# Gathering the chosen rows at the end of the ranking stage instead of at the start of the transformer stage

## The chip, the cores and the metric

The kernel runs on one core of a Trainium2 chip. The metric is the device time of one execution in microseconds (us). The program is one launch that runs seven stages one after the other. Names used below: PE is TensorE, DVE is VectorE, ACT is ScalarE, POOL is GpSimd, and SP is SyncE, which only issues DMAs here.

## What is computed

Input x is 4 batches of 1024 tokens of 1024 features, all float32. Two blocks are applied.

```python
x = x + tanh(g_xattn) * mamba(ctx, z=_layernorm(x))        # a selective scan
x = x + tanh(g_ffn) * mixture_of_depths(_layernorm(x))
# inside mixture_of_depths:
scores = einsum('btd,d->bt', hidden_states, w_router)
_, idx = top_k(scores, k)            # k = 128 of the 1024 tokens of a batch
idx = sort(idx)
sel = hidden_states[b, idx]          # 4 x 128 rows
...                                  # rotary attention at positions idx, MLP, gate
output = hidden_states.at[b, idx].set(gated)
```

So each batch ranks its tokens, the 128 best of each batch go through one transformer layer (16 query heads, 8 key heads of 128, causal over all 512 chosen rows), and their results are written back to their places. Every other row gets only the layer norm part.

## The kernel before

The stages, in order, are `project_stage`, `scan_stage` for batches 0 and 1, `route_stage` and `layer_stage` for batches 0 and 1 (`first = 0`), `scan_stage` for batches 2 and 3, and `route_stage` and `layer_stage` for batches 2 and 3 (`first = 2`). Each stage is a block in which every engine has a program of its own, written out by hand; engines meet only at semaphores. A stage ends when all five engines have come to its end: the code between two stages is a barrier of all engines, and no instruction or DMA of the next stage is issued ahead of it. SP is the last of them here, since its program ends with waits for all DMAs of the stage. This kernel therefore has two places, called boundaries below, at which a ranking stage hands over to a transformer stage.

`route_stage` (names with `r_`) reads the rows of both batches (`r_x`), computes each row's score, and ranks by comparing: `rank(b, a)` on DVE counts for 128 tokens how many scores of the batch are larger, `choose(b)` marks those with fewer than 128. `place(b)` gives each chosen token its slot (a PE product `p_sums`, then four small dependent DVE operations), `choose_slots(b)` builds eight 128x128 selection matrices `pick[:, a]` on DVE (in `first = 0` they lie in a part of `t_hidden`), and PE multiplies them with the positions held in `counts`, adding up in `p_pos` the sorted positions of the 128 chosen tokens, one on each partition. `copy_pos(b)` copies them to `r_pos`. The positions of batch b = 0 of the stage are done within the ranking of b = 1. Those of b = 1 are the stage's last work: SP waits for them, writes them to a scratch tensor in HBM and waits for that store.

`layer_stage` (names with `l_`) starts by loading the positions back (`l_pos`), then small tables, the router row and `tg` (the two gates), and then the weight ring `l_ring`, all from SP in that order:

```python
sp.dma_start(pos[:], t["pos"][:, 0:KEYS]).then_inc(pos_in, 16)
for dst, src in ((cols, t["cols"]), (swap, t["swap"]), (router, t["router"].partition_broadcast(P)),
                 (tg, t["g"].partition_broadcast(P))):
    sp.dma_start(dst[:], src).then_inc(small, 16)
```

DVE turns the positions into int32 row numbers (`from_i` for rows of this stage, `row_i` for the final write, `pos_i` for the rotary table). POOL waits for all three (`idx_ready, 3`) and issues four indirect DMAs: two gather 128 rows of 4 KB each (`l_rows`), two gather 128 rows of 1 KB each of the rotary table (`l_ropes`). DVE takes statistics of the rows (L1883), POOL raises them to the power -1/2 (L1646), ACT normalises (L1783, after a tanh of `tg` that stands ahead of it, L1780), PE transposes (L1675), ACT and DVE copy the transposed tiles out (L1790, L1900, which need `cols`), and PE begins the query and key products (L1686), each of 24 weight tiles of 512 KB. From there the layer is a long row of PE products.

Of the kernel before, what the change touches and what calls it, by code (L numbers as in the profile page):

```python
# [24 lines left out]
P = 128  # L25
# [13 lines left out]
SPAN = 2  # L39
# [22 lines left out]
class Through:  # L62

    def __init__(self, nc, ctx):
        self.hidden = ctx.enter_context(nc.sbuf_tensor("t_hidden", [P, NI, ROWS], F32))

class Kept:

    def __init__(self, nc, ctx, through):
        self.hidden = through.hidden
# [1005 lines left out]
def route_stage(nc, t, ctx, keep, first):  # L1079
# [34 lines left out]
    pos = sb("pos", [P, SPAN])  # L1114
# [12 lines left out]
    if late:  # L1127
# [3 lines left out]
        w_x = sb("w_x", [P, NE, ND])  # L1131
# [9 lines left out]
    slots, pick_ready, pos_sums, pos_done = (sem(n) for n in ("slots", "pick_r", "pos_sums", "pos_done"))  # L1141

# [6 lines left out]
    with nc.Block() as block:  # L1149
        @block.sync  # L1150
        def _(sp):
# [57 lines left out]
        def _(pool):  # L1209
# [72 lines left out]
        def _(pe):  # L1282
# [42 lines left out]
            for b in range(SPAN):  # L1325
# [15 lines left out]
        def _(dve):  # L1341
# [113 lines left out]
def layer_stage(nc, t, ctx, keep, first):  # L1455
# [22 lines left out]
    rows = sb("rows", [P, SPAN, DI])  # L1478
# [14 lines left out]
    ropes = sb("ropes", [P, SPAN, 2 * DH])  # L1493
# [28 lines left out]
    small, made, pos_in, idx_ready, k0_in, v0_in = (sem(n) for n in ("small", "made", "pos_in", "idx", "k0_in", "v0_in"))  # L1522
    x_in, rope_in = ([sem(f"{n}_in{b}") for b in range(SPAN)] for n in ("x", "rope"))
# [28 lines left out]
    with nc.Block() as block:  # L1552
        @block.sync
        def _(sp):
            sp.dma_start(pos[:], t["pos"][:, 0:KEYS]).then_inc(pos_in, 16)
# [73 lines left out]
        def _(pool):  # L1629
# [25 lines left out]
            if last_half:  # L1655
                for b in range(NB):
# [10 lines left out]
        def _(pe):  # L1667
# [30 lines left out]
            for r in range(2):  # L1698
                for b in range(SPAN):
                    if r == 0:  # L1700
                        pe.wait_ge(rope_in[b], 16)
                    last = nc.tensor.transpose(acc[3][:, r * ROWS + b * P:r * ROWS + (b + 1) * P], ropes[:, b, r * DH:(r + 1) * DH], ident[:])
# [165 lines left out]
        def _(dve):  # L1868
            dve.wait_ge(pos_in, 16)
            nc.vector.tensor_copy(pos_i[:], pos[:]).then_inc(idx_ready, 1)  # L1870
            for b in range(KEYS):
                nc.vector.tensor_scalar(row_f[:, b:b + 1], pos[:, b:b + 1], float(b * L), None, ALU.add)
            for b in range(SPAN):
                last = nc.vector.tensor_scalar(from_f[:, b:b + 1], pos[:, first + b:first + b + 1], float(b * L), None, ALU.add)
            last.then_inc(stat_chain, 1)
            dve.wait_ge(stat_chain, 1)
            nc.vector.tensor_copy(from_i[:], from_f[:]).then_inc(idx_ready, 1)
            nc.vector.tensor_copy(row_i[:], row_f[:]).then_inc(idx_ready, 1)

            for b in range(SPAN):  # L1880
                dve.wait_ge(x_in[b], 16)
                for h in range(H2):
                    nc.vector.bn_stats(stats[:, b, 6 * h:6 * h + 6], halves(rows[:, b], h)).then_inc(stat_chain, 1)  # L1883
            for b in range(SPAN):
                dve.wait_ge(stat_chain, 1 + H2 * (b + 1))
# [53 lines left out]

            dve.wait_ge(rope_ready, 1)  # L1940
# [81 lines left out]
SCRATCH = dict(pre=(SPAN * NE * P, L), ug=(STEPS * P, 2 * L), xd=(NB * ND, L), x2_0=(SPAN * L, DI), x2_2=(SPAN * L, DI), pos=(P, NB), k0=(P, NKV * ROWS), v0=(P, SPAN * DI),  # L2022
               h2T0=(P, KT * ROWS), base0=(ROWS, DI), coef0=(P, SPAN), mlp0=(ROWS, DI))
SCRATCH_KIND = "Internal"
STAGES = ((project_stage,), (scan_stage, 0), (route_stage, 0), (layer_stage, 0), (scan_stage, SPAN))
# [73 lines left out]
```

## Time and profile before

| | us |
|---|---|
| median of 3 runs | 2959.4 (2956.54 to 2963.68) |
| the profiled execution's own time | 2957.47 |
| its span, first to last recorded instruction | 2955.7 |
| PE busy | 2411.5 (82%) |
| DVE busy | 2043.6 (69%) |
| ACT busy | 1637.1 (55%) |
| POOL busy | 1637.4 (55%) |
| DMA, mean of the span | 142 GB/s |

All trace times are counted from the start of the span. The busy shares are means over stages with different limits, so what a change at one boundary is worth is read in the stretch around it. The first ranking stage ends near 1099 us, the second near 2331 us.

### The profile page before, as it was taken

What the parts mean: (1) busy time and instruction counts of PE and PEld (TensorE: products, weight loads), DVE (VectorE), ACT (ScalarE), POOL (GpSimd) and SP (SyncE); (2) the same over time, 40 slices, a digit from 0 to 9 for tenths busy, and PEclk for the clock granted to TensorE, in tenths of its full rate; (3) what the DMA queues carried; (4) which work ended last, traced back from release to release, by engine and by line L of the source; (5) the groups of instructions that cost most, each with busy time, mean ns of one, the idle gap of its engine ahead of it and who ended that gap; (6) DMA issues with size and microseconds to landing.
All of it is one profiled execution on the core that took longest, in us unless ns stands there. A gap on an engine that the chain in (4) does not pass through costs nothing. (4 is left out here: it accounts for less than half of the span.)

```text
span 2955.7 us, 33859 instructions
## 1 busy us (share of the span) xinstructions
PE 2411.5 (82%) x11576; PEld 1657.1 (56%) x11576; DVE 2043.6 (69%) x2562; ACT 1637.1 (55%) x3494; POOL 1637.4 (55%) x728
## 2 busy tenths in 40 slices
PE   8858778787777548986888888887886699999998
PEld 3335555555555317554666666666553486568863
DVE  4559999999999754433998999999996533210000
ACT  3468888888888342244887777887772213310000
POOL 1169999999999410004998998998991100000000
PEclk9979999999999768997999999999997799999999
DMA  6722252342522486744226325325326742244442
GB/s 262 239 88 75 65 162 79 105 138 65 164 65 61 181 343 225 281 146 149 90 80 196 97 92 177 100 90 185 95 63 264 261 135 79 68 143 153 150 156 100
DMA packets 237818, 418.62 MB, mean 142 GB/s; under 512 B 34512, under 2 KB 118736, under 8 KB 234832
## 3 DMA queue, kind: packets, MB, share of 16 engines
q1 hardware_dynamic: 224144, 360.36, 37.7%
q10 hardware_dynamic: 12160, 51.39, 4.3%
q0 software_dynamic: 1344, 4.72, 0.4%
q8 instruction: 93, 1.52, 0.2%
q14 instruction: 77, 0.63, 0.1%
HBM read 332.52 MB, written 83.89 MB: 141 GB/s over the span
## 5 line engine op out<-in xcount | busy, mean ns | idle before, releaser
L629 POOL TENSOR_TENSOR s_x<-s_du,k_bB 128x2048 f32<-128x2048 f32 (+1 forms) x256 | 882.0, 3458 | 29.9 <-issue 23.2
L705 PE MATMUL s_py<-k_ident,s_x 128*128 128x128 f32 x4096 | 564.1, 283 | 181.0 <-DVE s_x L1010 104.7
L705 PEld LDWEIGHTS s_py<-k_ident,s_x 128*128 128x128 f32 x4096 | 478.9, 145 | 401.4 <-DVE s_x L1010 179.4
L956 ACT ACTIVATE s_pA<-s_delta,k_negA 128x512 f32<-128x512 f32 x768 | 500.2, 681 | 184.4 <-DVE s_x L1010 179.3
L636 POOL TENSOR_TENSOR s_x<-s_hp,k_bC 128x1024 f32<-128x1024 f32 x192 | 452.9, 2373 | 26.6 <-DVE s_hp L1029 26.5
L1686 PE MATMUL l_p<-l_hT,l_ring 128*128 128x256 f32 x1792 | 397.2, 381 | 2.4 <-DVE l_hT L1900 1.4
L1010 DVE TENSOR_TENSOR s_x<-s_pA,k_bC 128x1024 f32<-128x1024 f32 x320 | 384.4, 1201 | 4.6 <-DMA k_bC<-scratch_xd 4.4
L1686 PEld LDWEIGHTS l_p<-l_hT,l_ring 128*128 128x128 f32 x1792 | 342.1, 191 | 50.2 <-issue 2.0
L856 ACT ACTIVATE s_xT<-s_duT,k_BT 128x128 f32<-128x128 f32 x1024 | 335.9, 387 | 0.1
L1029 DVE TENSOR_TENSOR_SCAN s_pA<-s_pA,s_x 128x512 f32<-128x512 f32 x256 | 302.4, 1215 | 40.3 <-ACT s_pA L956 40.1
L1029 DVE TENSOR_TENSOR_SCAN s_pA<-s_pA,s_carry,s_x 128x512 f32<-128x512 f32 x256 | 316.5, 1270 | 0.3
L694 PE MATMUL s_pA<-k_ident,s_xT 128*128 128x128 f32 x1024 | 152.6, 297 | 93.8 <-DVE s_hp L1029 90.3
L1693 PE MATMUL l_p<-l_ring,t_hidden 128*128 128x512 f32 x512 | 220.2, 592 | 0.0
L1654 POOL TENSOR_TENSOR l_squares<-l_squares,l_minus_half 128x1 f32<-128x1 f32 x4 | 2.2, 548 | 382.0 <-DVE l_squares L1990 382.0
L694 PEld LDWEIGHTS s_pA<-k_ident,s_xT 128*128 128x128 f32 x1024 | 122.7, 151 | 148.8 <-DVE s_hp L1029 146.9
L1663 POOL DMA_INDIRECT out_dram<-l_rows,l_row_i x2 | 1.9, 952 | 331.1 <-DVE l_rows L2017 331.1
L956 ACT ACTIVATE s_x<-s_delta,k_negA 128x512 f32<-128x512 f32 x256 | 169.8, 708 | 0.0
L1693 PEld LDWEIGHTS l_p<-l_ring,t_hidden 128*128 128x128 f32 x512 | 97.1, 190 | 121.1 <-issue 121.0
L1029 DVE TENSOR_TENSOR_SCAN s_hp<-s_pA,s_carry,s_x 128x512 f32<-128x512 f32 x128 | 161.9, 1265 | 4.2 <-ACT s_pA L956 4.2
L2012 DVE TENSOR_TENSOR t_hidden<-l_silu,l_p 128x256 f32<-128x256 f32 x32 | 13.5, 421 | 208.4 <-PE l_p L1686 208.4
L1029 DVE TENSOR_TENSOR_SCAN s_hp<-s_pA,s_x 128x512 f32<-128x512 f32 x128 | 154.8, 1209 | 1.9 <-ACT s_pA L956 0.6
L755 PE MATMUL s_p_in<-t_hidden,s_w_in 128*128 128x512 f32 x256 | 136.7, 617 | 0.0
(213 smaller groups left out, 3721.8 us busy)
## 6 DMA issues: line engine op xcount, KB each, us to landing
k_bC<-scratch_xd SPq DMA_DIRECT2D x32, 1024.0 KB, 9.5
scratch_ug<-p_ug ACTq DMA_DIRECT2D x16, 1024.0 KB, 3.9
k_u<-scratch_ug SPq DMA_DIRECT2D x64, 256.0 KB, 3.4
k_bB<-scratch_xd SPq DMA_DIRECT2D x16, 1024.0 KB, 9.2
s_gy<-scratch_ug SPq DMA_DIRECT2D x64, 256.0 KB, 4.4
s_xt<-in_x SPq DMA_DIRECT2D x64, 256.0 KB, 4.7
scratch_x<-s_xt SPq DMA_DIRECT2D x64, 256.0 KB, 2.3
r_x<-scratch_x SPq DMA_DIRECT2D x32, 512.0 KB, 12.5
```

The lines of the kernel that those rows point to most:

```text
L629: pool.tensor_tensor(out=x[:, 4 * g:4 * g + many], in0=du[:, s % 2:s % 2 + 1].broadcast_to([P, many, HALF]), in1=bB[:, 3 * g + g % 2:3 * g ...
L636: pool.tensor_tensor(out=x[:, 2 * i:2 * i + 2], in0=hp[:, POOL_PAIRS.index(i)], in1=bC[:, 2 * i:2 * i + 2], op=ALU.mult).then_inc(pool_hc, 1)
L694: last = nc.tensor.transpose(pA[:, n % 4, a * P:(a + 1) * P], xT[:, k, a * P:(a + 1) * P], ident[:])
L705: last = nc.tensor.matmul(py[:, a], x[:, n, a * P:(a + 1) * P], ident[:], is_transpose=True, start=False, stop=is_last and a == HALF // P - 1)
L755: last = nc.tensor.matmul(p_in[:], w_in[:, s % 2, i], ctxT[:, chunk(s) % 2, i], start=i == 0, stop=i == NK - 1)
L856: last = nc.scalar.activation(xT[:, k, a * P:(a + 1) * P], duT[:, a * P:(a + 1) * P], ACT.Copy, scale=BT[:, chunk(s) % 2, k, a:a + 1])
L956: nc.scalar.activation(out, delta[:, s % 2], ACT.Exp, scale=negA[:, s % NE, n:n + 1]).then_inc(dA_ready, 1)
L1010: nc.vector.tensor_tensor(x[:, 2 * i:2 * i + 2], pA[:, j:j + 2], bC[:, 2 * i:2 * i + 2], ALU.mult).then_inc(vec_hc, 1)
L1029: nc.vector.tensor_tensor_scan(out, dA, added, initial, ALU.mult, ALU.add).then_inc(scanned, 1)
L1686: last = nc.tensor.matmul(out[:, 0:ROWS], w[:, c * P:(c + 1) * P], src[:, c], start=c == 0, stop=c == KT - 1)
L1693: last = nc.tensor.matmul(banks[2 * a + h][:], src[:, a * P:(a + 1) * P], w[:, h * HALF:(h + 1) * HALF], start=is_first, stop=is_last)
L2012: nc.vector.tensor_tensor(hidden[:, m], silu[:, m % 2], acc[2 + m % 2][:, 0:ROWS], ALU.mult).then_inc(act_ready, 1)
```

## The change

The gathers move from the start of `layer_stage` to the end of `route_stage`, and their results live in tensors that both stages share.

- A class `Chosen` allocates `rows` and `ropes` (names `c_rows`, `c_ropes`) for each pair of a ranking and a transformer stage. `layer_stage` uses them in place of its own.
- The positions of all batches stay in SBUF, in `t_pos`. The scratch tensor, SP's store of it and SP's load of it are gone.
- `copy_pos(b)` makes the row numbers itself: one operation becomes four on DVE, and the second of them waits for the first.
- POOL's program in `route_stage` gets, for each batch, a wait for `from_i` and the gather of the rows, and a wait for `pos_i` and the gather of the rotary rows. SP waits for all four at the stage's end.
- Each of the eight selection matrices raises `pick_ready` by itself, and PE waits for each one ahead of its product, where it had waited for all eight.
- In the last stage the row numbers of the final write are made on DVE after `coefficients()`'s definition and ahead of the wait for the rotary table; before, they were made at the start of both transformer stages.
- `w_x` of the first ranking stage moves into a free part of `t_hidden`.

```diff
+class Chosen:
+    def __init__(self, nc, ctx, first):
+        self.rows = ctx.enter_context(nc.sbuf_tensor(f"c{first}_rows", [P, SPAN, DI], F32))
+        self.ropes = ctx.enter_context(nc.sbuf_tensor(f"c{first}_ropes", [P, SPAN, 2 * DH], F32))
...
 # route_stage, SP
-            sp.wait_ge(pos_done, SPAN)
-            sp.dma_start(t["pos"][:, first:first + SPAN], pos[:]).then_inc(small, 16)
-            sp.wait_ge(small, 64)
+            for b in range(SPAN):
+                sp.wait_ge(gathered[b], 32)
...
 # route_stage, POOL
+            for b in range(SPAN):
+                pool.wait_ge(idx_ready, b + 1)
+                pool.indirect_dma_start(out=chosen_rows.rows[:, b], out_offset=None, in_=t[f"x2_{first}"],
+                                        in_offset=bass.IndirectOffsetOnAxis(ap=from_i[:, b:b + 1], axis=0)).then_inc(gathered[b], 16)
+                pool.wait_ge(pos_done, b + 1)
+                pool.indirect_dma_start(out=chosen_rows.ropes[:, b], out_offset=None, in_=t["rope"],
+                                        in_offset=bass.IndirectOffsetOnAxis(ap=pos_i[:, b:b + 1], axis=0)).then_inc(gathered[b], 16)
...
 # route_stage, PE
-                pe.wait_ge(pick_ready, b + 1)
                 if b:
                     pe.wait_ge(pos_done, b)
                 for a in range(TILES):
+                    pe.wait_ge(pick_ready, TILES * b + a + 1)
                     last = nc.tensor.matmul(p_pos[:], pick[:, a], counts[:, P + a:P + a + 1], start=a == 0, stop=a == TILES - 1)
...
 # route_stage, DVE
             def choose_slots(b):
                 dve.wait_ge(slots, 4 * b + 4)
+                if b:
+                    dve.wait_ge(pos_sums, b)
                 for a in range(TILES):
-                    last = nc.vector.tensor_scalar(pick[:, a], counts[:, 0:P], slot[:, a:a + 1], chosen[:, b, a:a + 1],
-                                                   ALU.is_equal, ALU.mult)
-                last.then_inc(pick_ready, 1)
+                    nc.vector.tensor_scalar(pick[:, a], counts[:, 0:P], slot[:, a:a + 1], chosen[:, b, a:a + 1],
+                                            ALU.is_equal, ALU.mult).then_inc(pick_ready, 1)
             def copy_pos(b):
                 dve.wait_ge(pos_sums, b + 1)
-                nc.vector.tensor_copy(pos[:, b:b + 1], p_pos[:]).then_inc(pos_done, 1)
+                nc.vector.tensor_scalar(from_f[:, b:b + 1], p_pos[:], float(b * L), None, ALU.add).then_inc(from_ready, 1)
+                dve.wait_ge(from_ready, b + 1)
+                nc.vector.tensor_copy(from_i[:, b:b + 1], from_f[:, b:b + 1]).then_inc(idx_ready, 1)
+                nc.vector.tensor_copy(pos[:, first + b:first + b + 1], p_pos[:])
+                nc.vector.tensor_copy(pos_i[:, b:b + 1], p_pos[:]).then_inc(pos_done, 1)
...
 # layer_stage, SP, POOL, DVE
-            sp.dma_start(pos[:], t["pos"][:, 0:KEYS]).then_inc(pos_in, 16)
...
-            pool.wait_ge(idx_ready, 3)
-            for b in range(SPAN):
-                pool.indirect_dma_start(out=rows[:, b], out_offset=None, in_=t[f"x2_{first}"],
-                                        in_offset=bass.IndirectOffsetOnAxis(ap=from_i[:, b:b + 1], axis=0)).then_inc(x_in[b], 16)
-            for b in range(SPAN):
-                pool.indirect_dma_start(out=ropes[:, b], out_offset=None, in_=t["rope"],
-                                        in_offset=bass.IndirectOffsetOnAxis(ap=pos_i[:, first + b:first + b + 1], axis=0)).then_inc(rope_in[b], 16)
...
-            dve.wait_ge(pos_in, 16)
-            nc.vector.tensor_copy(pos_i[:], pos[:]).then_inc(idx_ready, 1)
...
+            if last_half:
+                for b in range(KEYS):
+                    last = nc.vector.tensor_scalar(row_f[:, b:b + 1], pos[:, b:b + 1], float(b * L), None, ALU.add)
+                last.then_inc(row_chain, 1)
+                dve.wait_ge(row_chain, 1)
+                nc.vector.tensor_copy(row_i[:], row_f[:]).then_inc(row_chain, 1)
             dve.wait_ge(rope_ready, 1)
```

The instructions move as follows. First DVE, at the first boundary, from the last selection matrices on. Before (the two branches are the end of one stage and the start of the next; the matrices go to a part of `t_hidden`):

```order
L1404 TENSOR_SCALAR t_hidden<-r_counts,r_slot,r_chosen 128x128 x8
L1410 COPY r_pos<-r_ppos 128x1
L1149 UNCONDITIONAL_BRANCH
L1867 UNCONDITIONAL_BRANCH
L1870 CAST l_pos_i<-l_pos 128x2
L1872 TENSOR_SCALAR l_row_f<-l_pos 128x1 x2
L1874 TENSOR_SCALAR l_from_f<-l_pos 128x1 x2
L1877 CAST l_from_i<-l_from_f 128x2
L1878 CAST l_row_i<-l_row_f 128x2
L1883 BN_STATS l_stats<-l_rows 128x6 x4
```

And with the change:

```order
L1425 TENSOR_SCALAR t_hidden<-r_counts,r_slot,r_chosen 128x128 x8
L1430 TENSOR_SCALAR r_from_f<-r_ppos 128x1
L1432 CAST r_from_i<-r_from_f 128x1
L1433 COPY t_pos<-r_ppos 128x1
L1434 CAST r_pos_i<-r_ppos 128x1
L1162 UNCONDITIONAL_BRANCH
L1876 UNCONDITIONAL_BRANCH
L1880 BN_STATS l_stats<-c_rows 128x6 x4
```

The row numbers are now made ahead of the two branches, and the statistics L1880 are the first DVE work of the transformer stage; the `l_row` operations are gone from this stage.

Second, POOL at the same boundary, from the last work of the ranking stage (the power of the variances) on. Before:

```order
L1224 TENSOR_TENSOR r_rstd<-r_var,r_minus_half 128x8 x2
L1149 UNCONDITIONAL_BRANCH
L2033 ISA
L1628 UNCONDITIONAL_BRANCH
L1630 MEMSET l_minus_half 128x4
L1631 MEMSET l_ident 128x128
L1632 MEMSET l_causalT 128x128
L1634 AFFINE_SELECT l_ident<-l_ident 128x128
L1636 AFFINE_SELECT l_causalT<-l_causalT 128x128
L1640 DMA l_rows<-scratch_x_0,l_from_i 128x1024 x2
L1643 DMA l_ropes<-in_rope,l_pos_i 128x256 x2
L1646 TENSOR_TENSOR l_roots<-l_roots,l_minus_half 128x4
```

And with the change:

```order
L1236 TENSOR_TENSOR r_rstd<-r_var,r_minus_half 128x8 x2
L1239 DMA c_rows<-scratch_x_0,r_from_i 128x1024
L1242 DMA c_ropes<-in_rope,r_pos_i 128x256
L1239 DMA c_rows<-scratch_x_0,r_from_i 128x1024
L1242 DMA c_ropes<-in_rope,r_pos_i 128x256
L1162 UNCONDITIONAL_BRANCH
L2033 ISA
L1645 UNCONDITIONAL_BRANCH
L1647 MEMSET l_minus_half 128x4
L1648 MEMSET l_ident 128x128
L1649 MEMSET l_causalT 128x128
L1651 AFFINE_SELECT l_ident<-l_ident 128x128
```

The four indirect DMAs now stand ahead of the barrier (the ISA row), with the rotary rows of a batch behind its own rows; the `l_` memsets and L1656 follow one another without a DMA between.

## Rows read from the trace of the kernel before

**Rows 1.** Chain that ended last, second boundary: start us, us, what.

```profile
2331.07 1.98 DMA l_pos<-scratch_pos
...
2334.16 1.05 POOL l_rows L1640
2335.20 0.30 issue
2335.51 9.72 DMA l_rows<-scratch_x,l_from_i
...
2345.25 1.29 DVE l_stats L1883 x2
...
2348.51 1.25 ACT l_normed_rows L1783
...
2354.72 7.14 PE l_p L1686 x32
```

**Rows 2.** Timeline, first boundary: start us, us, engine, line, operation.

```profile
1088.18 0.15 DVE L1410 COPY r_pos<-r_ppos 128x1 f32<-128x1 f32 x1
...
1089.80 0.17 DVE L1395 TENSOR_TENSOR_SCAN r_upto<-r_ones,r_sums 128x8 f32<-128x8 f32 x1
1090.00 0.17 DVE L1397 TENSOR_TENSOR r_slot<-r_upto,r_sums 128x8 f32<-128x8 f32 x1
...
1090.41 2.14 DVE L1404 TENSOR_SCALAR t_hidden<-r_counts,r_slot,r_chosen 128x128 f32<-128x128 f32 x8
...
1092.60 3.58 PE L1337 MATMUL r_ppos<-r_counts,t_hidden 128*128 128x1 f32 x16 [3.05 <-DVE t_hidden L1404]
...
1096.40 0.32 SPq L1197 DMA_DIRECT2D scratch_pos<-r_pos  x1
...
1099.05 0.32 SPq L1555 DMA_DIRECT2D l_pos<-scratch_pos  x1
...
1100.83 0.48 SPq L1558 DMA_DIRECT2D l_tg<-in_g  x1
...
1105.12 0.20 ACT L1780 ACTIVATE l_tg<-l_tg 128x2 f32<-128x2 f32 x1 [15.84 <-DMA l_tg<-in_g]
...
1111.29 1.29 DVE L1883 BATCH_NORM_STATS2 l_stats<-l_rows 128x6 f32<-128x512 f32 x2 [9.98 <-DMA l_rows<-scratch_x,l_from_i]
1113.86 1.29 DVE L1883 BATCH_NORM_STATS2 l_stats<-l_rows 128x6 f32<-128x512 f32 x2 [1.28 <-DMA l_rows<-scratch_x,l_from_i]
...
1117.11 2.37 ACT L1783 ACTIVATE l_normed_rows<-l_rows,l_shift,l_roots 128x1024 f32<-128x1024 f32 x2 [11.78 <-DVE l_shift L1893]
...
1123.32 5.05 PE L1686 MATMUL l_p<-l_hT,l_ring 128*128 128x256 f32 x21 [0.33 <-DVE l_hT L1900]
```

**Rows 3.** Timeline, end of the second ranking stage.

```profile
2324.66 3.58 PE L1337 MATMUL r_ppos<-r_counts,r_pick 128*128 128x1 f32 x16 [3.05 <-DVE r_pick L1404]
...
2328.46 0.34 SPq L1197 DMA_DIRECT2D scratch_pos<-r_pos  x1
```

**Rows 4.** Busy time by stretch: stretch, engines, granted clock, DMA share, GB/s.

```profile
1094.00:1096.00 2.00, 2.00 (x11) 2.00 (x10) 0.00 (x0) 0.00 (x0) 0.00 (x0) 0.50 0.00 0
1106.00:1108.00 2.00, 0.00 (x0) 0.00 (x0) 0.00 (x0) 0.00 (x0) 0.56 (x1) 0.50 1.02 418
```

**Rows 5.** DMA issues, 1095 to 1130 us: KB each, median us to landing.

```profile
l_rows<-scratch_x,l_from_i POOLq DMA_INDIRECT x2, 10.2
l_ropes<-in_rope,l_pos_i POOLq DMA_INDIRECT x2, 10.1
...
scratch_pos<-r_pos SPq DMA_DIRECT2D x1, 1.0 KB, 1.4
...
l_tg<-in_g SPq DMA_DIRECT2D x1, 1.0 KB, 4.3
```

**Rows 6.** Tile l_ring, first six loads of layer 0.

```profile
DMA to landing us min/median/max: 6.4/10.7/13.1
```

**Rows 7.** DMA issues, last 11 us of the span.

```profile
out_dram<-l_rows,l_row_i POOLq DMA_INDIRECT x2, 3.4
```

More of the change, by code:

```diff
@@ L66, in __init__ @@
         self.hidden = ctx.enter_context(nc.sbuf_tensor("t_hidden", [P, NI, ROWS], F32))
+        self.pos = ctx.enter_context(nc.sbuf_tensor("t_pos", [P, NB], F32))
+class Chosen:
+    def __init__(self, nc, ctx, first):
+        self.rows = ctx.enter_context(nc.sbuf_tensor(f"c{first}_rows", [P, SPAN, DI], F32))
+        self.ropes = ctx.enter_context(nc.sbuf_tensor(f"c{first}_ropes", [P, SPAN, 2 * DH], F32))
 class Kept:
     def __init__(self, nc, ctx, through):
-        self.hidden = through.hidden
+        self.hidden, self.pos = through.hidden, through.pos
         def sb(name, shape):
@@ L1076, with route_stage @@
 DOWN_PARTS = (14, 26)
-def route_stage(nc, t, ctx, keep, first):
+def route_stage(nc, t, ctx, keep, chosen_rows, first):
     TILES, BUFS = L // P, SPAN * L // P
@@ L1113, in route_stage @@
     slot = sb("slot", [P, TILES])
-    pos = sb("pos", [P, SPAN])
+    pos = keep.pos
+    from_f = sb("from_f", [P, SPAN])
+    from_i = ctx.enter_context(nc.sbuf_tensor(f"r{first}_from_i", [P, SPAN], I32))
+    pos_i = ctx.enter_context(nc.sbuf_tensor(f"r{first}_pos_i", [P, SPAN], I32))
     p_row = [ctx.enter_context(nc.psum_tensor(f"r{first}_prow{j}", [P, L], F32)) for j in range(2)]
@@ L1130, in route_stage @@
         pick = space[:, (LATE_BUFS + 1) * L:(LATE_BUFS + 2) * L].rearrange("p (a c) -> p a c", c=P)
-        w_x = sb("w_x", [P, NE, ND])
+        w_x = space[:, (LATE_BUFS + 2) * L:(LATE_BUFS + 2) * L + NE * ND].rearrange("p (e c) -> p e c", c=ND)
         xd = space[:, LATE_BUFS * L:LATE_BUFS * L + SPAN * HALF].rearrange("p (b l) -> p b l", b=SPAN)
@@ L1141, in route_stage @@
     slots, pick_ready, pos_sums, pos_done = (sem(n) for n in ("slots", "pick_r", "pos_sums", "pos_done"))
+    from_ready, idx_ready, gathered = sem("from_r"), sem("idx_r"), [sem(f"gathered{b}") for b in range(SPAN)]
     def buf(k):
@@ L1452, with layer_stage @@
 LATE, LATE_FROM, LATE_QK = 4, 4, 10
-def layer_stage(nc, t, ctx, keep, first):
+def layer_stage(nc, t, ctx, keep, chosen_rows, first):
     QK = NH + NKV
@@ L1476, in at_least @@
             eng.wait_ge(s, n)
-    rows = sb("rows", [P, SPAN, DI])
+    rows, ropes, pos = chosen_rows.rows, chosen_rows.ropes, keep.pos
     hid = sb("hid", [P, SPAN, DI])
@@ L1520, in layer_stage @@
     acc, side = banks[0:4], banks[4:8]
-    small, made, pos_in, idx_ready, k0_in, v0_in = (sem(n) for n in ("small", "made", "pos_in", "idx", "k0_in", "v0_in"))
-    x_in, rope_in = ([sem(f"{n}_in{b}") for b in range(SPAN)] for n in ("x", "rope"))
+    small, made, row_chain, k0_in, v0_in = (sem(n) for n in ("small", "made", "row_chain", "k0_in", "v0_in"))
     stat_chain, means, var_ready, roots_ready, shift_ready = (sem(n) for n in ("stat", "means", "var", "roots_r", "shift_r"))
@@ L1655, in _ @@
             if last_half:
+                pool.wait_ge(row_chain, 2)
                 for b in range(NB):
@@ L1868, in _ @@
         def _(dve):
-            dve.wait_ge(pos_in, 16)
-            nc.vector.tensor_copy(pos_i[:], pos[:]).then_inc(idx_ready, 1)
-            for b in range(KEYS):
-                nc.vector.tensor_scalar(row_f[:, b:b + 1], pos[:, b:b + 1], float(b * L), None, ALU.add)
             for b in range(SPAN):
[L1874 to L1881, printed above, removed]
                 for h in range(H2):
@@ L2020, in _, with run, choose_and_attend @@
                         last.then_inc(rows_ready, 1)
-SCRATCH = dict(pre=(SPAN * NE * P, L), ug=(STEPS * P, 2 * L), xd=(NB * ND, L), x2_0=(SPAN * L, DI), x2_2=(SPAN * L, DI), pos=(P, NB), k0=(P, NKV * ROWS), v0=(P, SPAN * DI),
+SCRATCH = dict(pre=(SPAN * NE * P, L), ug=(STEPS * P, 2 * L), xd=(NB * ND, L), x2_0=(SPAN * L, DI), x2_2=(SPAN * L, DI), k0=(P, NKV * ROWS), v0=(P, SPAN * DI),
                h2T0=(P, KT * ROWS), base0=(ROWS, DI), coef0=(P, SPAN), mlp0=(ROWS, DI))
 SCRATCH_KIND = "Internal"
-STAGES = ((project_stage,), (scan_stage, 0), (route_stage, 0), (layer_stage, 0), (scan_stage, SPAN))
-LAST_STAGES = ((route_stage, SPAN), (layer_stage, SPAN))
 def build(nc, t):
-    def run(stages, keep):
-        for stage, *which in stages:
-            with nc.cleanup_on_exit(), ExitStack() as ctx:
-                stage(nc, t, ctx, keep, *which)
+    def run(stage, *args):
+        with nc.cleanup_on_exit(), ExitStack() as ctx:
+            stage(nc, t, ctx, *args)
+    def choose_and_attend(keep, first):
+        with ExitStack() as half:
+            chosen_rows = Chosen(nc, half, first)
+            run(route_stage, keep, chosen_rows, first)
+            run(layer_stage, keep, chosen_rows, first)
     with ExitStack() as whole:
@@ L2038, in build @@
         with ExitStack() as outer:
-            run(STAGES, Kept(nc, outer, through))
-        run(LAST_STAGES, through)
+            keep = Kept(nc, outer, through)
+            run(project_stage, keep)
+            run(scan_stage, keep, 0)
+            choose_and_attend(keep, 0)
+            run(scan_stage, keep, SPAN)
+        choose_and_attend(through, SPAN)
 def kernel(x, ctx_1024, g_xattn, g_ffn, L0_xattn_in_proj_w, L0_xattn_conv_w, L0_xattn_conv_b, L0_xattn_x_proj_w,
```

9 lines of the change are left out of this document (1 added, 8 removed).

## The prediction

> **What bounds the kernel now.** I read the chain of work that ended last first, because the busy shares are means over seven unlike stages. At the second boundary [rows 1] the reader is to see that it runs through no busy engine: the position load, the making of row numbers, POOL's first gather and the wait for the second, then statistics, normalisation, and at 2354.72 PE's query products. From the stage's start at 2331.07 to there are 23.65 us, 9.72 of them one gather. The timeline of the first boundary [rows 2] shows the same: SP's position load at 1099.05, statistics at 1111.29 and 1113.86 (the second waited for its gather), L1686 at 1123.32, which is 24.27 us. Everything behind these two points follows from them: each boundary has one chain, each stage waits for the stage before, so what a boundary gains the span gains.
>
> The gathers are slow in company. Their median from issue to landing is 10.2 us for rows of 4 KB and 10.1 us for rows of 1 KB [rows 5]; a quarter of the bytes took as long, while the DMA engines moved 418 GB/s [rows 4] with the weight ring queued beside them. The final scatter, 512 KB by the same kind of issue and alone, landed in 3.4 us [rows 7].
>
> **The change part by part.** Call S the start of the transformer stage, E the end of the position products of b = 1, and S' and E' the same points with the change.
>
> *The position products.* PE needed 3.58 us for its 8 products of b = 1 at both boundaries [rows 2, 3], at the lower clock (granted 0.50, that is 1.2 GHz, after a stretch without work) [rows 4]; that is 0.45 us each. DVE makes eight matrices in 2.14 us, 0.27 each [rows 2], so PE sets the pace once it may follow. It starts after the first matrix, some 0.3 us, instead of after 2.14: 1.8 us gained. Seven more waits cost between nothing and what PE took after the last matrix (1092.55 to 1092.60, 0.05 each, 0.35 together); I take nothing, since a wait whose matrix is ready long before holds nobody.
>
> *The longer `copy_pos(0)`.* It stands between the ranking and `choose(1)` on DVE at 1088.18, on the chain. One copy becomes four operations. The second depends on the first, and such a step took 0.20 us (1089.80 to 1090.00) [rows 2]; each of the other two costs between nothing and the copy's 0.15. I take 0.4 us in all. So E' = E − 1.8 + 0.4 = E − 1.4.
>
> *The gathers of b = 0* are issued from about 1089 on, five us ahead of those of b = 1. DVE and PE work covers them; their 640 KB last 1.5 us at 418 GB/s. Without that cover they would cost what those of b = 1 do.
>
> *From E' to the stage's end.* First two DVE steps, 0.4 us, then 0.3 us until POOL issues, as between its issues [rows 1], then the row gather, which held POOL 1.05, another 0.3, then the rotary gather: issued at E' + 2.05. SP waits for its landing, D later. The barrier took 1.25 us: the store of the positions, at 1096.40, landed 1.4 later, at 1097.8, and the stage began at 1099.05 [rows 2, 5]. S' = E' + 3.3 + D. Before, S was 2.87 after E (1092.60 + 3.58 to 1099.05), and 2.83 at the second boundary, where the store at 2328.46 follows in the same way [rows 2, 3]. Together, S' − S = D − 0.95.
>
> *D* has no row, since no gather ran alone. From below, a 1 KB store landed in 1.4 us; from above, the gathers took 10.1 beside the weights [rows 5]. The nearest row is the scatter's 3.4 [rows 7], and 384 KB less at 418 GB/s take off 0.9. The barrier forbids any weight load beside it, so I take 2.8 us, between the two. Then S' = S + 1.85. The rows of b = 1, issued 1.35 earlier, land first even at 3.4.
>
> The Trainium skill has a price for such a DMA ("DMA: Bandwidth & Descriptors", Anatomy of one DMA): about 2.0 us and the bytes at 436 GB/s. By it D is 2.3, the forecast 1 us lower, and the trace agrees with it for the scatter (3.2 against 3.4). It disagrees with 10.1 for a gather, unless company explains that.
>
> *From S' to the query products.* The rows are there. Statistics of two tiles take two times 1.29 less a small overlap [rows 2], 2.5; from their end to the normalisation were 1.97 (2346.54 to 2348.51) [rows 1]. So ACT has its scale at S' + 4.6. But ACT's tanh of `tg` stands ahead of it in ACT's order: this is late next. `tg` was issued at 1100.83, 1.78 after S, the fifth issue; it becomes the fourth, 0.36 earlier. It lands 4.3 later [rows 5], at S' + 5.7; with 0.2 for the tanh, ACT normalises at S' + 6.0. I keep 4.3, since the router row, not the gathers, is queued ahead of it. From there to L1686 were 6.21 us at both boundaries [rows 1, 2]; those are dependent steps of PE, ACT and DVE, and stay. L1686 starts at S' + 12.2.
>
> The weights must be there too. SP issues the first at about S' + 1.9; the earliest of the first six landed after 6.4 us [rows 6], at S' + 8.3. It is covered by 3.9 us. Behind it, PE takes 3.57 us for a tile (7.14 for two) [rows 1] and 512 KB take 1.25 us at 418 GB/s, so the ring keeps ahead, in the last stage as well, where 4 MB of kept tensors follow.
>
> *At nothing:* the `row_f` and `row_i` operations in the last stage, six small ones while DVE waits for PE and ACT; the allocation of `w_x`.
>
> *Sum.* First boundary 24.27 − 12.2 − 1.85 = 10.2 us; second 23.65 − 12.2 − 1.85 = 9.6 us. Together 19.8 us. The profiled execution took 2957.5 us, so 2937.7; the median of the three runs is 1.9 above it, which gives 2939.6. I forecast 2939.
>
> **The rivals.**
>
> *A gather is slow by itself (7%).* For it: the two sizes landed alike. Against it: the scatter, and the 418 GB/s beside it. With D = 10.1, S' is 9.15 us later than S, the boundaries give 2.9 and 2.3 us, and the time is 2954, which this measurement can hardly tell from before (it tells 0.2%, 5.9 us).
>
> *Weights become the last to arrive (8%).* If the first tile landed as late as the slowest of six, 13.1 us [rows 6], L1686 would start at S' + 15.0, 2.8 later at each boundary: 2945. Against it: less is queued ahead of it than before.
>
> *POOL and DVE hold each other up (8%).* POOL's gathers of b = 0 now stand beside DVE's placing and its eight matrices. If DVE stood still for each of two POOL issues of 1.05 us [rows 1], `choose` to E' grows by up to 2.1 us at each boundary: 2944. For it speaks no row, since POOL gathered only while DVE was idle. The Trainium skill ("SBUF — State Buffer", SBUF: two separate sides) says that the two engines share a port pair that one holds for a whole instruction, and that such DVE work keeps POOL from writing descriptors. In the second form only the gathers of b = 0 are late, which are covered; no run here shows either yet.
>
> *Slower (3%).* SP's wait for the last rotary gather now stands ahead of the barrier, and behind it are queued all table and weight loads. Before, a late gather had these beside it. The gain of a boundary is 12.1 us less S' − S, so it is gone at D = 13, and D = 16 gives about 2965. Longer landings than 10.1 in an emptied machine would need a cost that no row shows.
>
> *Another cause (4%)*, such as the moved addresses of tensors in the scan stages: no row prices it; I spread it over all three.
>
> **How the numbers follow.** The forecast has 70%. Its own range: D from 1.4 to 3.4 moves it by −2.8 to +1.2, the landing of `tg` by 1 us at each boundary, the waits on PE by +0.7, and the median of three runs by some 3: 2934 to 2944. With the weights and the POOL case, 86% lie from 2933 to 2948, which is the range; I leave out the slow gather. Faster by over 0.2% is 0.87 (these three and a part of the last), within 0.2% 0.09, slower 0.04.
>
> **What would show it.** In the profile after: the position products beginning some 0.4 us after the first matrix and lasting about 3.6; a rotary gather landing near 2.8 us, with the next stage starting about 1.25 behind it, near 1100.9; statistics within 0.2 us of that start; a tanh near S' + 5.8 as ACT's last wait before the normalisation; L1686 near 1113.1 and 2345. The prediction is wrong if D is far above 3.4, if L1686 waits for the ring, or if the scan stages change their length.

## The result and the profile after

The changed kernel took 2937.9 us, median of 5 runs (2934.8 to 2944.8), against 2957.8 for the kernel before on the same chip (2955.5 to 2963.7). The ratio is 0.993, 95% interval 0.9914 to 0.9947: 20.7 us less, somewhere from 15.7 to 25.4. The forecast was 2939. The profiled execution took 2935.34 us.

The page of the profile after, its span and its busy row:

```profile
span 2933.6 us, 33860 instructions
PE 2400.6 (82%) x11576; PEld 1647.5 (56%) x11576; DVE 2043.5 (70%) x2563; ACT 1636.6 (56%) x3494; POOL 1636.5 (56%) x728
```

The busy time of DVE, ACT and POOL hardly moved; 22.1 us of span are gone. PE's busy time is 10.9 us shorter here (it was 2411.5), but in a second trace of the same kernel (e0, below) it is 2410.0 with nearly the same span, 2935.3, so that is not the gain. It was waiting that went, and the timeline of the first boundary shows which (start us, us, engine, line, operation, in brackets the idle time before and what ended it):

```profile
1088.01 0.15 DVE L1430 TENSOR_SCALAR r_from_f<-r_ppos 128x1 f32<-128x1 f32 x1
1088.19 0.15 DVE L1432 CAST r_from_i<-r_from_f 128x1 int32<-128x1 f32 x1
...
1088.39 0.16 DVE L1408 TENSOR_SCALAR r_chosen<-r_larger 128x8 f32<-128x8 f32 x1
...
1090.13 0.95 POOL L1242 DMA_INDIRECT c_ropes<-in_rope,r_pos_i  x1 [0.30 <-issue]
...
1090.48 2.14 DVE L1425 TENSOR_SCALAR t_hidden<-r_counts,r_slot,r_chosen 128x128 f32<-128x128 f32 x8
...
1090.97 3.54 PE L1356 MATMUL r_ppos<-r_counts,t_hidden 128*128 128x1 f32 x16 [1.35 <-DVE t_hidden L1425]
...
1095.17 0.94 POOL L1239 DMA_INDIRECT c_rows<-scratch_x,r_from_i  x1 [4.09 <-DVE r_from_i L1432]
1096.41 0.95 POOL L1242 DMA_INDIRECT c_ropes<-in_rope,r_pos_i  x1 [0.30 <-issue]
1101.42 0.10 POOL L1647 MEMSET l_minus_half<- 128x4 f32 x1 [4.06 <-POOLq L2033]
...
1101.46 2.47 DVE L1880 BATCH_NORM_STATS2 l_stats<-c_rows 128x6 f32<-128x512 f32 x4 [6.43 <-PEq L2033]
...
1102.75 0.58 SPq L1575 DMA_DIRECT2D l_tg<-in_g  x1
...
1105.63 0.23 DVE L1890 SCALAR_TENSOR_TENSOR l_shift<-l_mv,l_roots 128x2 f32<-128x2 f32 x2 [1.16 <-POOL l_roots L1656]
1107.33 0.20 ACT L1789 ACTIVATE l_tg<-l_tg 128x2 f32<-128x2 f32 x1 [19.57 <-DMA l_tg<-in_g]
1107.44 2.36 ACT L1792 ACTIVATE l_normed_rows<-c_rows,l_shift,l_roots 128x1024 f32<-128x1024 f32 x2
...
1113.64 6.71 PE L1697 MATMUL l_p<-l_hT,l_ring 128*128 128x256 f32 x30 [1.01 <-DVE l_hT L1897]
```

L1880, L1792 and L1697 are the statistics, the normalisation and the query products, which were L1883, L1783 and L1686 [rows 2]. The transformer stage now starts 2.4 us later (1101.42 against 1099.05), but the statistics begin 0.04 us behind its start instead of 12.24, and the products begin 9.7 us earlier. From the stage's start to the products are 12.22 us instead of 24.28.

The DMA issues of 1094.6 to 1101 us, the two gathers of `b = 1` (median us to landing), and one row of those of 1101 to 1106:

```profile
c_rows<-scratch_x,r_from_i POOLq DMA_INDIRECT x1, 4.2
c_ropes<-in_rope,r_pos_i POOLq DMA_INDIRECT x1, 3.7
```
```profile
l_tg<-in_g SPq DMA_DIRECT2D x1, 1.0 KB, 4.6
```

A rotary gather of 128 KB that took 10.1 us beside the weights [rows 5] lands in 3.7. The chain that ended last of 2309 to 2336 us, the second boundary, answers to [rows 1]:

```profile
2324.64 4.14 DMA l_tg<-in_g
...
2328.80 0.20 ACT l_tg L1789
2329.01 1.14 ACT l_normed_rows L1792
...
2335.11 0.89 PE l_p L1697 x3
```

The gather that filled this chain for 9.72 us is out of it, and the landing of `tg` is in it, as the prediction said.

To account for the time I use marks of the traces. "Chosen" is the start of L1389 (after: L1408) for `b = 1`; "product" is the end of its position products; "start" is the stage's first instruction; "query" is the first query product.

| us, first / second boundary | chosen to product | product to start | start to query | chosen to query |
|---|---|---|---|---|
| before | 7.88 / 7.46 | 2.86 / 2.83 | 24.28 / 23.65 | 35.02 / 33.94 |
| after | 6.12 / 6.27 | 6.91 / 6.87 | 12.22 / 11.80 | 25.25 / 24.94 |

The sums fall by 9.77 and 9.00 us. The longer `copy_pos(0)`, ahead of "chosen", takes 0.26 of each back, so the boundaries gave 18.2 of the 22.1 us of span. The rest lies elsewhere: 0.2 ahead of the first boundary, 1.2 between the two, 2.5 behind the second. The 1.2 is within the scatter: the stretch from the first boundary's query products to the second "chosen" took from 1193.7 (e5) to 1200.7 us (e7) in the traces below. For the 2.5, busy time by stretch (PE, PEld, DVE, ACT, POOL, then granted clock, DMA share, GB/s) of nearly the same place in the last stage, and of the low clock in it, before and after:

```profile
2600.00:2650.00 50.00, 44.15 (x183) 36.18 (x182) 11.10 (x20) 9.26 (x16) 3.86 (x4) 0.90 0.40 135
2609.66:2618.90 9.24, 8.22 (x27) 6.95 (x28) 5.07 (x8) 3.95 (x6) 2.75 (x2) 0.50 0.10 41
```
```profile
2580.00:2630.00 50.00, 44.01 (x193) 36.37 (x192) 11.45 (x21) 9.25 (x16) 3.29 (x4) 0.97 0.45 145
2590.05:2593.20 3.15, 3.15 (x15) 3.15 (x16) 1.36 (x3) 1.70 (x3) 0.00 (x0) 0.50 0.00 0
```

In 50 us PE did 183 products before and 193 after, at a granted clock of 0.90 and 0.97 of 2.4 GHz. In both traces PE had been idle for 4.8 us (to 2609.66 and 2590.05) and went on at 0.50, for 9.2 us before and for 3.2 after. This is not the scatter of one execution. From the second boundary's first query product to the end of the span are 600.8 to 601.2 us in the kernel before, e1, e2, e4 and e5, and 598.3 to 598.6 in the changed kernel, e0, e3 and e6 to e10. So the 2.5 us come with the change each time, though neither part of it brings them alone (e1, e2). The prediction has no term for them, and why the low clock lasts shorter is open.

### The profile page after: what moved, and what is told of

It is laid out like the page before. It is cut to its first block and busy times, and to the rows that moved or that the text cites. A ratio compares the mean times of both kernels' runs of the same rounds, so it can differ in the third digit from the quotient of the medians.

```text
span 2933.6 us, 33860 instructions
## 1 busy us (share of the span) xinstructions
PE 2400.6 (82%) x11576; PEld 1647.5 (56%) x11576; DVE 2043.5 (70%) x2563; ACT 1636.6 (56%) x3494; POOL 1636.5 (56%) x728
## 5 line engine op out<-in xcount | busy, mean ns | idle before, releaser
L714 PE MATMUL s_py<-k_ident,s_x 128*128 128x128 f32 x4096 | 557.6, 281 | 179.2 <-DVE s_x L1019 106.7
L1697 PE MATMUL l_p<-l_hT,l_ring 128*128 128x256 f32 x1792 | 394.6, 379 | 2.9 <-DVE l_hT L1897 1.8
L1697 PEld LDWEIGHTS l_p<-l_hT,l_ring 128*128 128x128 f32 x1792 | 340.2, 190 | 49.7 <-issue 2.2
## 6 DMA issues: line engine op xcount, KB each, us to landing
k_bC<-scratch_xd SPq DMA_DIRECT2D x32, 1024.0 KB, 10.2
```

What stands on the lines that cost most here:

```text
L714: last = nc.tensor.matmul(py[:, a], x[:, n, a * P:(a + 1) * P], ident[:], is_transpose=True, start=False, stop=is_last and a == HALF // P - 1)
L1697: last = nc.tensor.matmul(out[:, 0:ROWS], w[:, c * P:(c + 1) * P], src[:, c], start=c == 0, stop=c == KT - 1)
```

## The experiments

All ratios are to the kernel before on the same chip, with 95% intervals. The marks are from the profiled execution of each.

| kernel | median us | ratio | chosen to product | product to start | start to query |
|---|---|---|---|---|---|
| e0_changed_again | 2936.22 | 0.9925 (0.9908 to 0.9942) | 6.13 / 5.93 | 6.92 / 6.71 | 13.03 / 11.88 |
| e1_follow_only | 2953.14 | 0.9988 (0.9979 to 0.9997) | 6.14 / 6.13 | 2.87 / 2.82 | 24.09 / 24.04 |
| e2_no_follow | 2942.30 | 0.9946 (0.9934 to 0.9959) | 7.85 / 7.84 | 6.80 / 6.74 | 12.14 / 12.06 |
| e3_router_last | 2940.16 | 0.9938 (0.9926 to 0.9951) | 6.12 / 6.27 | 6.91 / 6.74 | 11.86 / 12.17 |
| e4_weights_wait | 2948.24 | 0.9964 (0.9949 to 0.9978) | 7.87 / 7.70 | 2.88 / 2.82 | 18.66 / 19.50 |
| e5_pos_in_sbuf | 2949.75 | 0.9974 (0.9965 to 0.9982) | 7.88 / 7.46 | 1.47 / 1.40 | 21.82 / 22.22 |
| e6_cross | 2937.65 | 0.9935 (0.9920 to 0.9950) | 6.12 / 5.93 | 7.02 / 6.86 | 11.91 / 12.47 |
| e7_cross_router_last | 2941.06 | 0.9943 (0.9928 to 0.9958) | 6.13 / 6.28 | 6.93 / 6.92 | 11.90 / 12.26 |
| e8_company | 2940.34 | one execution | 6.13 / 6.27 | 6.90 / 9.82 | 12.22 / 12.26 |
| e9_tables_early | 2936.90 | 0.9933 (0.9918 to 0.9948) | 6.13 / 6.27 | 6.91 / 6.92 | 10.52 / 10.52 |
| e10_gathers_together | 2942.56 | 0.9948 (0.9934 to 0.9962) | 6.14 / 6.13 | 10.13 / 9.49 | 11.37 / 12.07 |

e0 is the changed kernel once more, on the chip of e8 to e10. It shows how far one kernel's marks scatter: 0.8 us from start to query.

> The changed kernel itself, on the same chip as the others of this group: ratio to before 0.993, for comparison.

### One part alone

**e1_follow_only** is the kernel before with this part of the diff alone, and **e2_no_follow** the changed kernel without it:

```
-                pe.wait_ge(pick_ready, b + 1)
...
+                    pe.wait_ge(pick_ready, TILES * b + a + 1)
...
+                if b:
+                    dve.wait_ge(pos_sums, b)
```

> The kernel before with one part of the change: each selection matrix raises the semaphore and PE follows each. Forecast's theory: PE at the lower clock sets the pace (0.45 us a product), so its 8 products of the second batch start after the first matrix and end 1.8 us earlier at each boundary; 3.6 us less than before, 2954 us on the scale of this pair's before, ratio 0.9988. Rival: eight waits cost PE what the overlap gives, or DVE is slowed by eight semaphore updates; then the matrices take more than 2.14 us or the products more than 3.6 us, and the time is that of before.

> The changed kernel without that part: PE waits for all eight matrices again. Forecast's theory: the two parts are independent, so it loses 1.8 us at each boundary against the changed kernel and keeps some 16.5 us against before, ratio 0.9944. Rival (the parts overlap, the following is hidden behind the gather): time of the changed kernel, ratio 0.993.

Both came out as expected. Following the picks takes 1.74 and 1.33 us off the products in e1; leaving it out of the changed kernel gives 1.73 and 1.57 back. With or without the gathers the part is worth the same at the boundaries. The whole time of e2 also has the 2.4 us of low clock in the last stage, so it isn't a measure of this part.

**e5_pos_in_sbuf** is the kernel before with positions that stay in SBUF, and gathers where they were:

```
-            sp.dma_start(t["pos"][:, first:first + SPAN], pos[:]).then_inc(small, 16)
-            sp.wait_ge(small, 64)
...
-            sp.dma_start(pos[:], t["pos"][:, 0:KEYS]).then_inc(pos_in, 16)
```

> The kernel before with one part of the change: positions stay in SBUF, no store and no load through HBM; the gathers stay at the start of the transformer stage. Theory: the stage starts 1.4 us earlier (the store's landing) and the row numbers are made 1.6 to 2.0 us earlier in it (the load's landing): 3.0 and 3.4 us, together 6.4, ratio 0.998. Since the gathers are then issued ahead of most weights, they may also land sooner, by up to 3 us each: then 0.996. Rival: the DMA engines are the bound of the first 12 us of the stage, so earlier gathers land no earlier: ratio 1.0.

The stage starts 1.4 us earlier, and from there to the query products go 2.5 and 1.4 us: 3.9 and 2.9 at the boundaries, 6.7 together where 6.4 were expected. Its gathers were still slow:

```profile
l_rows<-scratch_x,l_from_i POOLq DMA_INDIRECT x2, 8.9
l_ropes<-in_rope,l_pos_i POOLq DMA_INDIRECT x2, 8.8
```

So the round trip of the positions is a third of the gain, and the gathers' length is a matter of its own.

### Why the gathers were slow

**e4_weights_wait** is the kernel before, with the weight ring held until the gathers have landed:

```
+            for b in range(SPAN):
+                sp.wait_ge(x_in[b], 16)
+                sp.wait_ge(rope_in[b], 16)
             for n in range(SLOTS_W):
                 load(n)
```

> The kernel before, with gathers where they were, but SP issues the weight ring only after the four gathers have landed. Theory A (gathers took 8.5 to 10.7 us because weights were moved beside them): they land in 4 to 5 us, the query products start near 1117 and 2349, 6.4 and 5.4 us earlier, with the first weight tile landing about a microsecond ahead of need; 12 us less than before, ratio 0.996. Theory B (the gather is slow by its place after the barrier): they land in 9 to 10 us as before, the weights then come late, and the time is that of before or up to 10 us more.

The DMA issues of 1099 to 1125 us of e4:

```profile
l_rows<-scratch_x,l_from_i POOLq DMA_INDIRECT x2, 4.9
l_ropes<-in_rope,l_pos_i POOLq DMA_INDIRECT x2, 3.8
```

The same four gathers, at the same place, in 4.9 and 3.8 us instead of 10.2 and 10.1 [rows 5]. What made them slow was the company of the weight loads, not the gather. The kernel is 9.2 us faster than before by the median, where 12 were expected. PE does not wait for the ring: its first query product starts at 1121.35, released by DVE's copy, and the first ring load had landed at 1116.3. Start to query fell by 5.6 and 4.2 us, by as much as the second row gather lands earlier behind the start (9.2 and 10.0 us instead of 14.8 and 14.2).

**e10_gathers_together** is the changed kernel with the gathers of `b = 0` held back, so that all four stand on the path. One line goes in ahead of POOL's gathers:

```
+            pool.wait_ge(pos_done, SPAN)
```

> The changed kernel, but POOL issues the gathers of b = 0 only when the positions of b = 1 are made, so all four follow E'. Forecast's theory (those of b = 0 are hidden): now two more issues of 1.25 to 1.48 us stand ahead of the last rotary gather, and the stage ends 2.7 us later at each boundary; 5.4 us more than the changed kernel, ratio to before 0.995. Rival (POOL and DVE hold each other up when the gathers of b = 0 are issued beside DVE's matrices): part of that is won back, DVE's slot chain and matrices being shorter than in the changed kernel.

```profile
1096.02 1.18 POOL L1240 DMA_INDIRECT c_rows<-scratch_x,r_from_i  x1 [26.27 <-DVE r_pos_i L1435]
1097.51 0.95 POOL L1243 DMA_INDIRECT c_ropes<-in_rope,r_pos_i  x1 [0.30 <-issue]
...
1100.01 0.95 POOL L1243 DMA_INDIRECT c_ropes<-in_rope,r_pos_i  x1 [0.30 <-issue]
1105.34 0.10 POOL L1648 MEMSET l_minus_half<- 128x4 f32 x1 [4.38 <-POOLq L2034]
```

The timeline shows two more issues, 2.75 us, on the path, and the stage starts 3.2 and 2.6 us later than in the changed kernel. So the early gathers are worth about 3 us a boundary; the kernel takes 6.3 us more than e0 on the same chip, where 5.4 were expected. It also answers the rival of POOL and DVE: with no gather beside DVE's placing, chosen to product is 6.14 and 6.13, against 6.12 and 6.27 with two of them beside it.

### What ends the ranking stage

The prediction had SP's wait for the last landing hold the stage. **e6_cross** takes this wait away: indices and semaphores live on with the tensors, SP waits for the positions alone, and DVE and PE wait for the landings in the transformer stage.

```
-            for b in range(SPAN):
-                sp.wait_ge(gathered[b], 32)
+            sp.wait_ge(pos_done, SPAN)
...
+                        pe.wait_ge(chosen_rows.rope_in[b], 16)
...
+                dve.wait_ge(chosen_rows.row_in[b], 16)
```

> The changed kernel, but the ranking stage ends without waiting for the gathers to land: their semaphores and row numbers live across the barrier, DVE waits for each batch's rows and PE for each batch's rotary rows in the transformer stage. Theory (SP's wait for the last rotary gather, 3.7 us, is what the stage's end costs): the next stage starts when POOL has issued the last gather and the barrier is through, 2.7 us earlier, the rows of b = 1 land within its first microsecond, and ACT's wait for the small loads is last as before; 5.4 us less than the changed kernel, ratio to before 0.991. Rival (company slows the gathers again): the last gathers land 8 us or more after issue and the gain is gone.

The stage did not start earlier: 7.02 and 6.86 us behind the products, against 6.91 and 6.87. Timeline of e6, and its rotary gather's landing (tile `c_ropes`, 1095 to 1110 us):

```profile
1099.56 0.95 POOL L1243 DMA_INDIRECT c_ropes<-in_rope,c_pos_i  x1 [0.30 <-issue]
1104.68 0.33 SPq L1576 DMA_DIRECT2D l_cols<-in_cols  x1
1104.68 0.10 POOL L1648 MEMSET l_minus_half<- 128x4 f32 x1 [4.17 <-POOLq L2037]
```
```profile
DMA to landing us min/median/max: 3.8/3.8/3.8
```

It landed at 1103.3 and the stage started at 1104.68, 1.3 us behind it, though no wait that the kernel's text asks for joins the two. Either POOL's end of stage holds until its gathers have landed (A), or leaving a stage after such an issue has a fixed length (B). **e8_company** tells them apart. It is e6 with 2 MB of loads at the end of the second ranking stage, which nothing reads:

```
+            for n in range(4 if first else 0):
+                sp.dma_start(chosen_rows.ahead[:, n], t["wq"][n * P:(n + 1) * P, :]).then_inc(chosen_rows.ahead_in, 16)
```

> The kernel whose gathers cross the barrier, and in the second half SP issues four loads of 512 KB (2 MB, 5 us at 415 GB/s; never used) right when the last positions are made, which nobody waits for before the last stage's end. Theory A (what ends the ranking stage is POOL, whose last instructions there return only when its gathers have landed): the last gathers land 7 to 9 us after issue, and the transformer stage starts 1.3 us after that landing, 9.5 to 11 us after the last position product instead of 7.0. Theory B (POOL needs 4.1 us after its last issue whatever the DMAs do): the stage starts 7.0 us after the last product as before, and the gathers land after its start. Two MB of dead loads stand in this kernel, so its time is not compared.

```profile
2318.51 1.76 SPq L1216 DMA_DIRECT2D c_ahead<-in_wq  x4
2318.62 0.94 POOL L1245 DMA_INDIRECT c_rows<-scratch_x,c_from_i  x1 [4.39 <-DVE c_from_i L1438]
2319.86 0.95 POOL L1248 DMA_INDIRECT c_ropes<-in_rope,c_pos_i  x1 [0.30 <-issue]
2327.79 0.33 SPq L1581 DMA_DIRECT2D l_cols<-in_cols  x1
```

The tile `c_ropes` of 2300 to 2330 us, both rotary gathers of that stage:

```profile
DMA to landing us min/median/max: 4.6/5.6/6.7
```

The last rotary gather, issued at 2319.86, now takes 6.7 us and lands at 2326.5; the stage starts at 2327.79, 1.3 behind it and 9.82 behind the products. At the first boundary, without the loads, it is 6.90. So the gap follows the landing, as A has it, and B falls.

```profile
L1164 POOLq DRAIN  x1: 5332/5332/5332, 1098.2 to 1098.2; - x1
```
```profile
L1167 POOLq DRAIN  x1: 8195/8195/8195, 2318.5 to 2318.5; - x1
L1167 SPq DRAIN  x1: 7/7/7, 2321.0 to 2321.0; - x1
```

POOL's ends at 1103.6 and 2326.7, each 0.2 us behind the last gather's landing. SP's took 7 ns, though the first of its four added loads landed only at 2322.1 and the last at 2327.6. A is thus shown for gathers issued by POOL, and in e8 it does not hold for loads issued by SP.

### The small loads behind the start

`tg` is the last of four small loads on one semaphore, so ACT's tanh waits for all of them. **e3_router_last** (and **e7_cross_router_last**, the same on e6) puts `tg` first and the router row of 512 KB last:

```
-            for dst, src in ((cols, t["cols"]), (swap, t["swap"]), (router, t["router"].partition_broadcast(P)),
-                             (tg, t["g"].partition_broadcast(P))):
+            for dst, src in ((tg, t["g"].partition_broadcast(P)), (cols, t["cols"]), (swap, t["swap"]),
+                             (router, t["router"].partition_broadcast(P))):
```

> The changed kernel with the four small loads of the transformer stage in another order: tg first, the router row of 512 KB last. Theory: the wait that is late after the change is ACT's for these four loads, because tg is queued behind the router row. With the router last they have all landed some 4.6 us after the stage's start instead of 5.9, which is when the statistics chain is done as well (4.4 to 4.6); L1697 comes 1.3 us earlier at each boundary, 2.6 us less than the changed kernel, ratio to before 0.992. Rival: the four land as a group however they are ordered, no difference.

> Both: gathers cross the barrier, and the router row is the last of the four small loads. Theory: the two gains add, 5.4 and 2.6 us, because the statistics chain (4.5 us from the stage's start) still ends with the small loads; 8 us less than the changed kernel, ratio to before 0.990. Rival: the rows of b = 1 become the last to arrive and it is no faster than with the barrier crossed alone.

Neither gained. DMA issues of 1101 to 1112 us of e3, and its tanh:

```profile
l_router<-in_router SPq DMA_DIRECT2D x1, 512.0 KB, 4.2
...
l_tg<-in_g SPq DMA_DIRECT2D x1, 1.0 KB, 2.1
```
```profile
1107.50 0.20 ACT L1789 ACTIVATE l_tg<-l_tg 128x2 f32<-128x2 f32 x1 [20.61 <-DMA l_router<-in_router]
```

`tg` lands in 2.1 us when nothing is ahead of it. But now the router row is last and has the first ring loads beside it; it took 4.2 us (4.5 at the second boundary), where it took 3.3 and 3.5 in the changed kernel. What stands behind it in the queue goes with its length in the other runs too: 4.2 and 4.5 in e9, where the first ring load again follows 0.4 us behind it, and 3.1 in e4, where the ring is held. The wait moved from one load to the other. I had kept 3.3 for it, and that was the miss.

**e9_tables_early** takes three of the four out of the way: `cols`, `swap` and the gates are loaded in the ranking stage into tensors that live on, and ACT waits for no load.

```
+            for dst, src in ((chosen_rows.cols, t["cols"]), (chosen_rows.swap, t["swap"]),
+                             (chosen_rows.gates, t["g"].partition_broadcast(P))):
+                sp.dma_start(dst[:], src).then_inc(tables_in, 16)
...
-            act.wait_ge(small, 64)
```

> The changed kernel, with the column table, the swap matrix and the gates tg loaded during the ranking stage into tensors that live on; only the router row is left to load in the transformer stage, and nothing ahead of the query products waits for it. Theory: ACT's wait for the small loads (5.5 to 6.1 us after the stage's first load, whichever was last) is what the normalisation waits for in the changed kernel and in the router-last run; without it ACT starts when the statistics chain ends, 4.4 us after the start, and the query products come 1.4 us earlier at each boundary, 2.8 us in all, ratio to before 0.992. Rival: the tables were not it; the weights (issued 1.4 us earlier now) or the transposes are next at the same time, no difference to the changed kernel.

```profile
1099.83 0.10 POOL L1654 MEMSET l_minus_half<- 128x4 f32 x1 [4.07 <-POOLq L2038]
...
1104.30 2.37 ACT L1797 ACTIVATE l_normed_rows<-c_rows,l_shift,l_roots 128x1024 f32<-128x1024 f32 x2 [4.25 <-DVE l_shift L1895]
...
1110.35 7.14 PE L1704 MATMUL l_p<-l_hT,l_ring 128*128 128x256 f32 x32 [0.27 <-issue]
```

ACT normalises 4.47 us behind the start at both boundaries, released by the statistics' chain, and the query products start 10.52 behind it, 1.7 and 1.3 us earlier than in the changed kernel. The trace shows the expected 2.8 us or so; the times do not tell it from the changed kernel on the same chip (2936.9 and 2936.2). I call its mechanism shown and its gain not shown.

## Why the prediction was right, point by point

**The bound.** Right: what the boundaries' chains lost, the span lost. It lost 3.9 us more outside the boundaries, of which 2.5 are the shorter low clock of the last stage.

**The position products.** 1.8 us were forecast, 1.76 and 1.19 came. The products began 0.49 us behind the start of the first matrix and took 3.54. The second boundary gave less for a reason that has nothing to do with the matrices. PE's four small products for the slots, between "chosen" and the first matrix, took 0.39 and 0.37 us a pair before, at a granted clock of 1.00, and 0.59 and 0.57 after, at 0.50, so that the matrices began 2.09 us behind "chosen" instead of 1.69. From the start of the matrices to the end of the products 1.59 us were gained there. In e0 the same way to the matrices took 1.89. PE began 0.64 behind the start of the first matrix.

**The longer `copy_pos(0)`.** 0.4 forecast, 0.26 measured: from its first operation to `choose(1)` are 0.38 us, where it was 0.12.

**From E' to the start.** E' + 3.3 + D forecast. Without D it was 3.21 and 3.17. This term was right in size but incomplete in its reason. Besides SP's wait, POOL's own end of stage holds until its gathers land (e6, e8), and taking SP's wait away frees nothing.

**D.** This is the term that was mis-sized: 2.8 forecast, 3.7 measured at both boundaries, 0.9 too short each time. I had scaled the scatter's 3.4 us [rows 7] down by its bytes. The gathers don't scale so: 128 KB took 3.7 and 512 KB, issued just ahead, 4.2 and 4.3. By the fixed cost and the rate of the Trainium skill ("DMA: Bandwidth & Descriptors", Anatomy of one DMA) the estimate for these is 2.3 and 3.2 us; the trace disagrees by 1.4 and 1.0 us.

**From the start to the query products.** S' + 12.2 forecast, 12.22 and 11.80 measured, with tanh as ACT's last wait (S' + 5.9 and 5.5). The landing of `tg`, taken at 4.3, was 4.6 and 4.1. It scatters: 5.4 in e0. The statistics' own way to ACT, set at S' + 4.6, adds up to 4.5 (2.5 and 1.97), and e9 measured 4.47; nothing hung on it.

**The sum.** S' lies 4.05 − 1.76 + 0.26 = 2.55 us behind S at the first boundary and 4.04 − 1.19 + 0.26 = 3.11 at the second (product to start, chosen to product, the copy), where 1.85 was forecast. So the boundaries gave 24.28 − 12.22 − 2.55 = 9.5 and 23.65 − 11.80 − 3.11 = 8.7, so 18.2 instead of 19.8. D accounts for 1.8 of the difference. The shorter low clock in the last stage gave 2.5 us, more than that back. That the time came within about 1 us of the forecast is in that part luck: two errors of the sum nearly cancelled.

**The rivals.** *A gather slow by itself* fell with e4 and with D = 3.7. *Weights last* didn't come: the first ring load, issued at 1103.37, landed 6.5 us later at 1109.8, 3.8 ahead of L1697. *POOL and DVE hold each other up* fell: the eight matrices take 2.14 us with a rotary gather's issue across their start (1090.13 to 1091.08 beside 1090.48), as they did before with POOL idle [rows 2], and e10 gives the same length. POOL's row gather took 1.18 us there, but 1.18 in e10 as well, where DVE was done. Whether DVE's work delays the gathers of b = 0 themselves no run separates: beside it, the row gather and the rotary gather landed in 5.7 and 5.1 us at the first boundary, with ACT's stores of rows also on the DMA engines, and in 4.2 and 4.1 at the second. They were covered, as the prediction said. *Slower* needed D over 13; even with 2 MB beside it e8 shows 6.7. *Another cause*: the scan stages kept their length within the scatter (0.2 and 1.2 us), but the low clock of the last stage, which no rival names, took 2.5 us off.

## What to carry to other kernels

Look at what a slow gather shares the DMA engines with before blaming the gather: the same four took about 10 us with the weights queued beside them and 4 to 5 with the weights held back. Issue gathers as soon as their indices exist, ahead of the barrier that lets the bulk loads go, and count on the stage lasting until they have landed; in this kernel the next one starts 1.3 us behind that. When one load of a group is late, moving it forward in the queue helps only if the load that becomes the last isn't slowed by what now stands beside it.

## What the runs showed of the hardware

- A stage in which POOL has issued gathers doesn't end before they have landed, waited for or not. POOL's DRAIN at its end took 5.3 us in e6 and 8.2 in e8, to 0.2 us behind the last landing, and the next stage starts 1.3 to 1.4 us behind it. SP's DRAIN with four loads of its own under way took 7 ns (e8).
- With no loads beside them, a gather of 128 rows of 1 KB lands in 3.3 to 4.7 us, of 128 rows of 4 KB in 4.2 to 5.6 (e4, e6, e10, and those of b = 1 in the changed kernel). Beside 512 KB weight loads both took 8.3 to 10.7 (before, e5), and 6.7 to 7.0 beside four such loads (e8): company hid the size.
- A 1 KB broadcast load lands in 2.1 us when first (e3, e7), and in 3.3 to 5.4 behind a 512 KB one (e4 and e0, and all others between).
- Behind the same idle stretch of PE (4.8 us) at the same place of the last stage, the granted clock stayed at 0.50 for 9.2 us in the kernel before, 8.4 in e2, 4.4 in e0 and 3.2 in the changed kernel's first trace. The way from the query products to the end is 2.3 to 3.0 us shorter in all eight traces of kernels with both parts of the change than in the five others. That is more than several of the effects above, so those are read from the boundaries' marks and not from the whole time.
